# Score products over 32 rows of one image instead of 128 rows, of which 96 are zero

## The reference

```python
qkv = tokens @ w_qkv.T + b_qkv
q, k_, v = jnp.split(qkv, 3, axis=-1)
hd = C // NH                                   # 32 // 8 = 4
q, k_, v = (heads(q), heads(k_), heads(v))     # B, 8, 192, 4
scores = jnp.einsum('bhqd,bhkd->bhqk', q, k_) * (1.0 / np.sqrt(hd)).astype(x.dtype)
attn = jax.nn.softmax(scores, axis=-1)
o = jnp.einsum('bhqk,bhkd->bhqd', attn, v)
```

## Time and profile before

| | |
|---|---|
| median of 3 runs | 1162.87 us (1157.21 to 1165.39) |
| span of the profiled execution | 1225.6 us |
| PE busy | 971.3 us, 79% |
| DVE, ACT, POOL busy | 68%, 63%, 52% |
| score passes (L646) | 768, 172.2 us busy |
| granted TensorE clock, mean | 0.884 |

### The profile page before, as it was taken

One profiled execution on the slowest core, in us unless ns is written; L12 is line 12 of the kernel. 1 busy time (PEld: TensorE's weight loads), 2 busy tenths in 40 slices (PEclk: granted clock), 3 DMA queues, 4 the chain that ended last, 5 costly groups with the idle time before them and its releaser, 6 DMA issues.

```text
span 1225.6 us, 21628 instructions
## 1 busy us (share of the span) xinstructions
PE 971.3 (79%) x6440; PEld 762.4 (62%) x6440; DVE 835.0 (68%) x2114; ACT 774.3 (63%) x1899; POOL 631.8 (52%) x851
## 2 busy tenths in 40 slices
PE   3986865689888988898889889986786786488676
PEld 2765643577667766776678667865664565366544
DVE  5345776488558967896879677976694676455644
ACT  2545644486547786877688768875866575267543
POOL 4333316632665368546854576557516655562352
PEclk8998988799879999999899999998987589699855
DMA  9998977555566989898989888965453555436778
GB/s 244 314 264 227 272 210 180 146 159 157 133 156 184 266 217 237 236 291 208 233 238 274 228 238 227 265 187 143 132 169 98 132 154 151 123 98 195 212 221 269
DMA packets 176252, 247.82 MB, mean 202 GB/s; under 512 B 65512, under 2 KB 71912, under 8 KB 176136
## 3 DMA queue, kind: packets, MB, share of 16 engines
q1 hardware_dynamic: 167944, 244.03, 71.9%
q0 software_dynamic: 8192, 2.40, 1.5%
HBM read 124.53 MB, written 121.80 MB: 201 GB/s over the span
## 4 chain that ended last, share of the span: by engine, by line
PE 38%; DVE 20%; ACT 12%; issue 9%; DMA 9%; another core or an unknown queue 6%; POOL 5%; SPq 1%; ACTq 0%; DVEq 0%; POOLq 0%
PE cv L527 10%; PE sc L646 7%; PE pp L659 4%; PE xb L511 4%; PE tr L561 3%; DVE res L1350 3%; ACT wgt L843 3%; PE ib L574 2%; ACT pr L872 2%; PE ms L675 2%; DMA table<-xt 2%; DMA X<-in_x 2%; DVE stats L1126 2%; DMA tok_pos<-in_pos,idx 2%
## 5 line engine op out<-in xcount | busy, mean ns | idle before, releaser
L527 PE MATMUL cv<-X,w_conv 128*128 128x330 f32 (+1 forms) x1024 | 302.2, 422 | 11.6 <-issue 5.9
L527 PEld LDWEIGHTS cv<-X,w_conv 128*128 128x128 f32 x1024 | 193.3, 203 | 45.9 <-issue 12.1
L843 ACT ACTIVATE wgt<-ib,eps_col,mom 128x440 f32<-128x440 f32 (+1 forms) x256 | 177.6, 701 | 46.3 <-DVE res L1350 22.0
L1145 DVE TENSOR_SCALAR_CACHE_REDUCE junk<-flat,th 128x379 bf16<-128x379 f32 x200 | 120.6, 603 | 115.3 <-ACT th L829 89.3
L511 PE MATMUL xb<-cst,X 128*110 128x128 f32 x900 | 153.7, 297 | 48.8 <-ACT xt L809 28.3
L646 PE MATMUL sc<-k_b,qm 128*128 128x192 f32 x768 | 172.2, 353 | 16.2 <-DVE pixf L1245 7.3
L1046 POOL TENSOR_SCALAR res<-res,mom 128x440 f32<-128x440 f32 (+1 forms) x152 | 96.0, 634 | 171.0 <-DVE res L1350 169.3
L1350 DVE SCALAR_TENSOR_TENSOR res<-tr,mom,wgt 128x440 f32<-128x440 f32 (+1 forms) x192 | 122.2, 641 | 71.4 <-PE tr L561 31.0
L809 ACT COPY xt<-xb 110x512 f32<-110x512 f32 x225 | 131.6, 585 | 58.9 <-PE xb L511 30.7
L872 ACT ACTIVATE pr<-sc,least 128x192 f32<-128x192 f32 x384 | 137.1, 415 | 31.0 <-DVE least L1314 18.6
L659 PE MATMUL pp<-cst,pr 128*96 128x128 f32 x768 | 122.5, 284 | 33.6 <-ACT pt L883 25.4
(11 more groups left out here) (170 smaller groups left out, 1534.2 us busy)
## 6 DMA issues: line engine op xcount, KB each, us to landing
table<-xt SPq DMA_DIRECT2D x240, 224.0 KB
rt<-table SPq DMA_DIRECT2D x240, 224.0 KB
out<-res SPq DMA_DIRECT2D x320, 137.5 KB
X<-in_x SPq DMA_DIRECT2D x64, 412.5 KB, 6.4
X<-in_x SPq DMA_DIRECT2D x64, 343.8 KB, 6.5
conv_rows<-cvr SPq DMA_DIRECT2D x64, 188.0 KB
y<-conv_rows SPq DMA_DIRECT2D x64, 165.4 KB
out<-res SPq DMA_DIRECT2D x64, 68.8 KB
```

The costliest lines, as they stand in the source:

```text
L527: last = mm(cv[:, 0:CUT[half]], w_conv[:, 4 * q + z], X[:, m % XI, at0:at0 + CUT[half]], start=z == 0, stop=z == 3)
L843: last = A(wgt[:, n % 2, at0:at0 + w], ib[:, at0:at0 + w], ACT.Identity, scale=mom[:, NB * g + b, 2:3], bias=eps_col[:, 1:2])
```

## The change

A unit now contracts over the 32 partitions of its own image: both operands are sliced to rows 32b to 32b+31. The keys stay in one tile of 192 columns, copied by one instruction over 128 partitions; the zeroed tile and its memset are gone.

```diff
-        k_b = sb("k_b", [128, NB, K])
+        k_t = sb("k_t", [128, K])
...
-                queries = qm[:].rearrange("p h q -> p (h q)")
+                rows = slice(C * b, C * b + C)
+                queries = qm[rows].rearrange("p h q -> p (h q)")
                 for t in range(2):
                     last = mm(sc[:, k % 2, K * t:K * t + K], queries[:, 256 * m + 128 * t:256 * m + 128 * t + 128],
-                              k_b[:, b, :], start=True, stop=True)
+                              k_t[rows], start=True, stop=True)
...
-                for b in range(NB):
-                    rows = slice(C * b, C * b + C)
-                    last = A(k_b[rows, b, :], sc[rows, 1, 0:K], ACT.Identity, bias=qk_bias[rows, 1:2])
-                last.then_inc(qk_cp, 1)
+                A(k_t[:], sc[:, 1, 0:K], ACT.Identity, bias=qk_bias[:, 1:2]).then_inc(qk_cp, 1)
...
-            for w in (imp_b, y7, zrow, k_b):
+            for w in (imp_b, y7, zrow):
                 gp.memset(w[:], 0.0)
```

## The result

The changed kernel takes 1227.86 us (median of 4 runs, 1226.17 to 1238.25) against 1162.35 us before: a ratio of 1.060, 95% interval 1.056 to 1.064. It is slower by 65.5 us, where 33.5 us were forecast.

The account below looks back on a forecast made before the run. PE was taken as the bound most of the time in the score stretches. 96 units at 0.37 us gave +35.5 us, the keys -2 us: +33.5 us on 1162.9, so 1196 us (+2.9%); 8 in 10 range 1170 to 1228 us.

Parts of the forecast that it names:

- PE bounds the stretches with scores, half of the units lie on the chain: Eight score stretches, 657 us: PE busy 88%; about 96 of 192 units on the chain, the others' added time absorbed by waits.
- A pass over 32 rows is no faster: Score passes of 192 columns: contracting over 32 rows instead of 128 brings no shorter pass, 0 us.
- Ways in and out, 0.37 us in a unit: Around each score unit: way in, way out and two open loads, 0.29 to 0.39 us; 96 units on the chain, +35.5 us.
- rival 2: Score units: three more weight loads of 0.10 us open in each; near end of its range 1228 us; chance 0.05.
- Keys: Key copy on ACT: one instead of four starts the first unit 0.7 us earlier in three groups, -2 us, bounds 0 and 10.
- the granted clock stays what it is: Stretches with scores: no clock term in the sum, granted clock there 0.87 to 0.96 before the change.
- Rival 3: Stretches with scores: clock falls because PE stands still twice in each unit, 59 us lost, 1255 us; chance 0.04.
- The sign that the prediction gave for being wrong: Score stretches: the forecast is wrong if the clock differs there by over 0.03; unit cost and slot growth were other signs.

Follow-up runs that it names:

- the first trace: The unchanged kernel, traced ahead of the prediction: span 1225.6 us, 63 us over the median of the runs, granted clock 0.884.
- the second: The unchanged kernel, traced again to get an execution near the median: 1153.8 us, span 1151.9 us, granted clock 0.906.

## Why the prediction was wrong

1. *PE bounds the stretches with scores, half of the units lie on the chain.* About right for the steady part: 120 units with 0.39 us each are 47 us of pauses, and 18.8 us arrived, 40% of them. PE's time without work there fell from 576.7 - 516.6 = 60.1 us to 595.5 - 551.3 = 44.2 us; the waits took 16 of the other 28 us. Some 5 us may be clock (0.97 instead of 0.96), the rest isn't accounted for.
2. *A pass over 32 rows is no faster.* Right: of the 0.84 us for a unit 0.10 are its open load and 0.09 the way out, which leaves 0.65 us for four passes, as before.
3. *Ways in and out, 0.37 us in a unit.* Right in size, place by place. What such pauses cost in time the two runs with single-column passes show: +23 us for 0.30 us in each unit, +61 us for 0.60. For 0.39 us that makes 30 us in proportion to the first, 34 us on the line between the two (an estimate); the forecast said 35.5 us.
4. *Later loads open (rival 2, 0.05): three more loads of 0.10 us open in each unit.* No run shows them. They would make a unit 1.14 us, and it takes 0.84; the sum of the forecast had no term for them, only the upper end of its range, 1228 us, was drawn from this rival.
5. *Keys.* The mechanism was right: the first unit of group 0 no longer waits for the copy but for POOL, as the row below shows (changed kernel, timeline of PE). The size was not: -9 us with 128 rows instead of -2 us. I had counted only what PE waits for the copy. That the rest is the time for which ACT is free sooner isn't shown: with POOL filling all blocks ACT is busy for 759.6 us, with one copy for 758.5, before for 768.6, and yet only one copy gained. POOL has 12 us more to do in the run with its blocks, which may have used the gain up. In the change itself no gain from the keys is left (1222.6 us with four copies, 1227.9 with one).

```profile
236.67 0.88 PE L647 MATMUL sc<-k_t,qm 32*128 32x192 f32 x4 [1.00 <-POOL qm L1036]
```

6. *The step that failed: the granted clock stays what it is, so the sum has no term for it.* Rival 3 had 4%, and its argument was that PE stands still twice in each unit. I looked for pauses in the earlier trace rows, where the clock held, and concluded that it would hold. But that stretch belongs to group 3, in which convolutions over 128 rows run beside the scores, and the pauses were not the question. The earlier trace rows had a hint: the lowest clock of the eight stretches, 0.87, is that of group 5 (855 to 936 us). The runs show for group 5: with more pauses, but 128 rows, the clock is 0.88; with 64 rows 0.80; in the three kernels with 32 rows there and no additional products 0.62 to 0.68. Nine more traces with 128 or 96 rows have 0.84 to 0.87; only the first trace has 0.79, where PE is without work for 30.7 us of group 5 against 25.3 us in the second. The sign that the prediction gave for being wrong, a clock that differs by over 0.03, came in groups 5 and 6. Of the 54.5 us in groups 5 to 7, pauses explain about 12 us (the run with one pass took 10.1 us more there, 352.6 us against 342.5, and the run with two 16.6 us); the other 42 us are left for the clock. The 140 us more at the low level are 70 us of lost work, and PE's time without work fell by 26 us there (84.6 to 58.6): 12 + 70 - 26 = 56 us, near the 54.5. In groups 5 and 6 the convolution has ended or ends; scores are the largest group of passes that are left (20.3 of PE's 66.0 us in group 6 before), and the change takes three quarters of the rows out of just these. That the rows are what the clock followed remains the author's reading.

So the loss of 65.5 us is made of some 30 to 34 us for the ways in and out, close to the forecast, and some 30 to 40 us of clock, for which the sum had nothing (31 to 36 us are the rest between the medians, 42 us the rest between the traces). A part stays open: the clock does not fall by the same amount in each run. With 32 rows in groups 5 to 7 it falls in group 5 (0.64) and is 0.80 in group 6 when the keys are copied four times, while with one copy group 6 has 0.57. What decides between the two was not settled, nor why the clock of groups 0 to 4 is lower with four copies. Nor do the runs separate the number of rows from the time that PE spends on products over 32 or 64 rows: the passes that made the pauses had one column only.

## What to carry to other kernels

A product over fewer rows of the array was no cheaper here: four passes of 192 columns took 0.65 us over 128 rows and 0.64 to 0.67 over 96, and over 32 or 64 rows, with products over the whole array around them, they paid a way in, a way out and two open weight loads besides, 0.39 us for 0.65 us of work. Zero rows may be worth keeping. When a change takes rows out of the passes, read the granted clock in the stretches where these passes are the largest part of PE's work, not in the stretch with the highest load.

## What the runs showed of the hardware

- Going from products over the whole array to products over 32 or 64 rows and back cost 0.09 to 0.10 us each way, and the first weight load after it was open (0.10 us for 128 float32 columns): a unit of 0.65 us became one of 0.84 us, and the four convolution passes behind it went from 1.11 to 1.31 us. Products over 96 rows had no such price (0.64 to 0.67 us for a unit, ratio 1.002).
- Not expected: two kernels with the same score passes and columns, one with 128 rows and more pauses (clock 0.88, 0.86, 0.76 in groups 5 to 7), one with 32 rows (0.68, 0.57, 0.70), were granted different clocks; 64 rows lay between in group 5 (0.80).
- Not expected: adding 31 us of PE work over 128 rows to the changed kernel did not make it longer (1222.9 against 1227.9 us); the clock of groups 5 and 6 was 0.78 and 0.82 instead of 0.68 and 0.57.
